# A two-layer decoder on one core: a batch's causal attention of the last block held until a later score unit of the wide text attention

## The chip, the cores and the metric

The kernel runs on one core of a Trainium2 chip. The metric is the device time of one execution in microseconds. Engines are called by their names: TensorE (PE in rows, its weight loads PEld), VectorE (DVE), ScalarE (ACT), GpSimd (POOL) and SyncE (SP), which starts the DMAs.

## The reference

Eight sequences of 112 tokens with 256 channels pass through two decoder layers of three blocks each, with a layer norm behind each block. The last two blocks matter here. Block 4 of the kernel's numbering is an attention to a text of 375 tokens with 16 heads 64 wide. Block 5 is a causal attention with 16 heads 16 wide, followed by a mixture of four experts. Cut to that, for every sequence b:

```python
def _L1_xattn_ref(x, cond, w_q, w_k, w_v, w_out, b_out):   # N_HEADS, D_HEAD = 16, 64
    attn = softmax(einsum('bqhd,bkhd->bhqk', q, k) * D_HEAD ** -0.5)
    return einsum('bhqk,bkhd->bqhd', attn, v).reshape(B, SQ, 1024) @ w_out + b_out

def _L1_ffn_ref(x, ...):                                    # HEADS, HD = 16, 16
    h = _rms(x, n1_w)
    q, k, v = _rms(heads(wq), qn_w), _rms(heads(wk), kn_w), heads(wv)
    attn = softmax(where(causal, q @ k.T * HD ** -0.5, -inf))
    x = x + zero_first_64((attn @ v) @ wo.T)
    xf = _rms(x, n2_w)
    return x + zero_first_64(sum(wts[:, e] * expert_e(xf)))

x = _layernorm(x + _L1_xattn_ref(x, ctx_768, ...))
x = _layernorm(x + _L1_ffn_ref(x, ...))
```

## The kernel before

The kernel is written as plans, one per stage. A plan is a list of units such as `("sc4", n)`, and every engine walks the same list and issues its own instructions of each unit, so the list is the order in all five queues. `step` says what a unit leaves on each engine's semaphore and a rough cost; `weave` (its loop is near the top of `build`) fills a list from several streams in turn: each stream is a generator that yields the units it wants placed, or `None` while it has to wait. `until(units)` yields `None` until these units stand in the list, and `rest(ns)` until the placed units' costs have grown by so much. These waits shape the order of the list alone. What an engine waits for on the chip is written in `tensor_s4`, `vector_s4` and so on, by semaphores.

Stage 4 is the one that matters. Its streams are woven by one call of `weave`:

```python
weave(s4_heads(), follow(s4_values, range(2, 2 * B)),
      follow(s4_out, range(B)), follow(s4_operands, range(B)), follow(s4_queries, range(2, B, 2)),
      follow(s5_operands, range(0, B, 2)), follow(s5_operands, range(1, B, 2)), s5_heads(), follow(s5_out, range(0, B, 2)),
      follow(s5_out, range(1, B, 2)),
      s5_split())
```

`s4_heads` places the wide heads of block 4: 64 score units `sc4`, eight per sequence b (HP = 8), each with two heads. A score unit is six matmuls on TensorE (L2604), two row maxima on VectorE (L2684) and two exponentials on ScalarE (L2653). One unit later `nm4` normalises on VectorE (L2691, L2695), two units later `trA4` and `trV4` transpose (TensorE L2612; copies on ScalarE L2645 and VectorE L2676), and three units later `av4` multiplies by the values (L2623). Behind eight of them, `s4_out` places `out` (16 matmuls with Wo, L398, in rows `psum<-w_Wo,s_attT`; on VectorE the sum and the moments, L636 to L645; on GpSimd one root, L693), then `norm` (L688) and `xT` (L587, L630), which turn the rows for block 5.

Block 5's attention of a sequence is placed among the units of later sequences. `s5_operands(b)`, which runs in one stream for even and one for odd b, places `rms5a` (ScalarE's sum of squares L2850, a copy on GpSimd L2978), `ms5a` (L2909, L2912, a root on GpSimd L2981), `qkv5` (twelve matmuls, L398, in rows `psum<-w_wq,x_ch`, `w_wk`, `w_wv`), `qkv5e` (ScalarE L2856 to L2859), `ms5` (VectorE's sums L2916 and L2919, then the reciprocal roots of all heads on GpSimd, L2985), after a rest `qk5` (VectorE's multiply with these roots, L2923), `qkT5` (four transposes, L2775) and `qkT5e` (ScalarE L2863 for q, VectorE L2929 for k). `s5_heads` then takes the sequence in four groups: two `s5` units (scores L2784, mask L2787) with a maximum per group, `mx5` (VectorE L2938), `s5e` (four exponentials, ScalarE L2871), `pT5` (four transposes L2793, a copy on VectorE L2943), two `av5` (L2803) and `oT5` (L2878). `s5_out` places `turn5` (L2810; VectorE L2949, L2951), `atT5` (L2815, L2882), `wo5` (L398, `w_wo,at5T`; L2956), `sqb5` (L2887), `msb5` (L2960; a root on GpSimd L2989), `xf5` (L2964; GpSimd L2993) and `xfT5` (L2825, L2892, L2895; GpSimd L2997). The units `split5` round the first experts' weights (L2831, L2836).

When all wide heads are placed, `ffnin` stands in the list: SyncE then loads the experts' weights, once the last `av4` is done. What is left of block 5's attention comes behind, and with the next stage the experts' matmuls (`psum<-xf,e_up` first), which need all of it. Score units are counted from 0 to 63.

Of the kernel before, what the change touches and what calls it, by code (L numbers as in the profile page):

```python
# [18 lines left out]
B, N, D = 8, 112, 256  # L19
# [11 lines left out]
HP = H // 2  # L31
# [126 lines left out]
def build(nc, ctx, a, out):  # L158
# [63 lines left out]
    def until(*units):  # L222
        while any(u not in placed for u in units):
            yield None

    def rest(ns):
        end = spent[0] + ns
        yield None
        while spent[0] < end and not hurry[0]:
            yield None  # L230
# [2203 lines left out]
    def until_banks(count):  # L2434

        while sum(all(name in r.value for r, name in freed) for freed in w4.freed) < count + 3:
            yield None
# [59 lines left out]
        return [("split5", name)]  # L2497

    def s5_operands(b):
        yield from until(("norm", 4, b), ("ones5",))  # L2500
        if b >= 2:
            yield from until(("turn5", b - 2))
        yield [("rms5a", b)]
        yield [("ms5a", b)]
        yield from until(("xTe", 4, b))
        yield from rest(REST / 2)
        yield from until_banks(2)
        rings["misc5"].take(("vv5", b), (A, ("v5", b)))
        yield [("qkv5", b)]
        yield [("qkv5e", b)]  # L2510
        yield [("ms5", b)]
        yield from rest(5500.0)
        if b == B - 1:
            yield from until(("pT5", b - 1, 1))
        yield [("qk5", b)]
        yield from rest(REST)
        yield from until_banks(1)
        yield [("qkT5", b)]
        yield [("qkT5e", b)]
# [57 lines left out]
    def s5_split():  # L2577
# [6 lines left out]
# [5 lines that stand above are left out]
# [869 lines left out]
```

## Time and profile before

| | us |
|---|---|
| median of 3 runs | 1171.46 |
| lowest and highest of them | 1166.77, 1177.46 |
| span of the profiled execution | 1165.0 |
| TensorE busy in it | 1001.8 (86%) |
| VectorE busy | 640.4 (55%) |
| ScalarE busy | 588.3 (50%) |
| GpSimd busy | 284.6 (24%) |

No time of the profiled execution other than its span is given. The busy shares are means over the whole program, in which this stage is about a third: the wide score units start at 661.7 us and the experts' first matmul at 1024.4. In timelines a row is a group of like instructions that follow each other: its start, how long it lasts, engine, line, operation, the tiles out and in, their shape, the count, and in brackets the idle time ahead of it with what ended it. Two rows of TensorE can overlap by some tenths, since matmuls are pipelined.

### The profile page before, as it was taken

What the parts mean: (1) busy time and instruction counts of PE and PEld (TensorE: products, weight loads), DVE (VectorE), ACT (ScalarE), POOL (GpSimd) and SP (SyncE); (2) the same over time, 40 slices, a digit from 0 to 9 for tenths busy, and PEclk for the clock granted to TensorE, in tenths of its full rate; (3) what the DMA queues carried; (4) which work ended last, traced back from release to release, by engine and by line L of the source; (5) the groups of instructions that cost most, each with busy time, mean ns of one, the idle gap of its engine ahead of it and who ended that gap; (6) DMA issues with size and microseconds to landing.
All of it is one profiled execution on the core that took longest, in us unless ns stands there. A gap on an engine that the chain in (4) does not pass through costs nothing.

```text
span 1165.0 us, 21556 instructions
## 1 busy us (share of the span) xinstructions
PE 1001.8 (86%) x8624; PEld 707.4 (61%) x8624; DVE 640.4 (55%) x1519; ACT 588.3 (50%) x1374; POOL 284.6 (24%) x292
## 2 busy tenths in 40 slices
PE   7996898887689988789998799889888897789995
PEld 4664565665388854456655676667666665447654
DVE  3246545666669833454455476776676664527003
ACT  5532565552468844344544354556555544465741
POOL 2521412100500033211112202221132124132733
PEclk9988889898989999899999988999999888679998
DMA  9341464102679785422252243313222105000001
GB/s 311 99 86 40 112 127 110 45 12 98 209 272 314 259 278 168 139 88 85 80 173 88 81 120 105 101 34 107 81 57 78 27 1 226 1 1 1 1 1 32
DMA packets 66676, 123.68 MB, mean 106 GB/s; under 512 B 11632, under 2 KB 41968, under 8 KB 62496
## 3 DMA queue, kind: packets, MB, share of 16 engines
q1 hardware_dynamic: 64528, 117.48, 33.0%
q0 software_dynamic: 2048, 4.82, 1.4%
q8 instruction: 68, 1.11, 0.4%
q14 instruction: 32, 0.26, 0.1%
HBM read 86.30 MB, written 35.92 MB: 105 GB/s over the span
## 4 chain that ended last, share of the span: by engine, by line
PE 56%; DVE 19%; ACT 11%; DMA 5%; issue 4%; POOL 4%; SPq 1%; another core or an unknown queue 0%; DVEq 0%; ACTq 0%; POOLq 0%
PE psum L398 38%; DVE s_p L2695 3%; ACT s_p L2653 3%; POOL rs L2985 2%; PE psum L2612 2%; DVE s_max L2684 2%; PE psum L2623 2%; PE psum L1369 2%; PE psum L2784 1%; DVE s_pT L2676 1%; PE psum L550 1%; DVE s_max L653 1%; PE psum L2173 1%; PE psum L2159 1%; PE psum L2604 1%
## 5 line engine op out<-in xcount | busy, mean ns | idle before, releaser
L2653 ACT ACTIVATE s_p<-psum,s_max 112x375 f32<-112x375 f32 x128 | 72.3, 569 | 87.6 <-DVE s_max L2684 87.6
L693 POOL TENSOR_TENSOR rstd<-meanvar,minus_half 112x1 f32<-112x1 f32 x40 | 23.1, 578 | 279.6 <-DVE meanvar L645 209.9
L653 DVE TENSOR_REDUCE s_max<-psum 112x2 f32<-112x750 f32 x64 | 59.4, 935 | 32.5 <-PE psum L550 31.4
L2985 POOL TENSOR_TENSOR rs<-ms,minus_half 112x32 f32<-112x32 f32 x8 | 43.5, 5442 | 110.3 <-DVE ms L2919 110.3
L398 PE MATMUL psum<-Wv,ctx 128*125 128x512 f16 x240 | 59.6, 392 | 11.2 <-ACT s_v L624 5.4
L398 PE MATMUL psum<-ctx,Wk 128*128 128x375 f16 x320 | 62.8, 331 | 5.0 <-ACT s_yT L2242 2.8
L2684 DVE TENSOR_REDUCE s_max<-psum 112x1 f32<-112x375 f32 x128 | 63.7, 539 | 2.3 <-PE psum L2604 2.1
L2612 PE MATMUL psum<-ident,s_p 112*125 112x112 f32 x384 | 61.4, 294 | 3.9 <-DVE s_p L2695 2.3
L609 ACT ACTIVATE s_k<-psum 128x375 f16<-128x375 f32 x64 | 31.2, 488 | 62.1 <-PE psum L398 59.5
L2604 PE MATMUL psum<-s_k,s_q 64*112 64x375 f16 x384 | 46.0, 345 | 17.0 <-ACT s_p L2653 6.5
L2612 PEld LDWEIGHTS psum<-ident,s_p 112*125 112x125 f32 x384 | 51.7, 198 | 13.7 <-DVE s_p L2695 3.9
L3303 POOL TENSOR_TENSOR hidden<-raw,hidden 128x448 f16<-128x448 f32 x44 | 45.6, 1036 | 54.4 <-ACT hidden L3186 52.7
L1431 ACT ACTIVATE s_pT<-psum 125x672 f32<-125x672 f32 x64 | 46.6, 730 | 22.8 <-PE psum L1357 21.2
L2623 PE MATMUL psum<-s_pT,s_v 125*64 125x112 f32 x768 | 53.9, 278 | 4.4 <-ACT s_attT L2661 4.4
L677 DVE SCALAR_TENSOR_TENSOR s_k<-psum,s_k 128x375 f16<-128x375 f32 x64 | 34.8, 546 | 36.2 <-ACT s_k L609 35.8
L624 ACT ACTIVATE s_v<-psum 125x512 f32<-125x512 f32 x48 | 28.3, 596 | 49.2 <-PE psum L398 33.4
L2623 PEld LDWEIGHTS psum<-s_pT,s_v 125*64 125x64 f32 x768 | 39.7, 143 | 20.1 <-issue 17.3
L398 PEld LDWEIGHTS psum<-Wv,ctx 128*125 128x125 f16 x240 | 32.1, 141 | 32.3 <-issue 9.6
L2695 DVE TENSOR_SCALAR s_p<-s_p,s_sum 112x375 f32<-112x375 f32 x128 | 49.3, 427 | 2.3
L3275 DVE SCALAR_TENSOR_TENSOR x_tok<-psum,wt,x_tok 112x192 f32<-112x192 f32 x32 | 12.6, 414 | 68.7 <-PE psum L398 68.6
L2645 ACT ACTIVATE s_pT<-psum 125x336 f32<-125x336 f32 x64 | 29.0, 453 | 38.3 <-PE psum L2612 38.2
L398 PE MATMUL psum<-x_ch,w_Wq 128*128 128x224 f32 x192 | 46.3, 382 | 2.1 <-ACT x_ch L630 1.5
(360 smaller groups left out, 2445.1 us busy)
## 6 DMA issues: line engine op xcount, KB each, us to landing
keys<-s_k SPq DMA_DIRECT2D x64, 187.5 KB, 2.2
s_k<-keys SPq DMA_DIRECT2D x8, 1500.0 KB, 7.6
values<-s_v SPq DMA_DIRECT2D x48, 224.0 KB
s_v<-values SPq DMA_DIRECT2D x16, 672.0 KB
raw_wg<-in_wg SPq DMA_DIRECT2D x8, 1024.0 KB, 6.6
raw_wu<-in_wu SPq DMA_DIRECT2D x8, 1024.0 KB, 7.1
raw_wd<-in_wd SPq DMA_DIRECT2D x8, 1024.0 KB
s_kd<-k_halves SPq DMA_DIRECT2D x48, 93.8 KB, 3.8
```

The source lines that it names most:

```text
L398: ins = TE.matmul(bank, left, right, start=i == 0, stop=last)
L653: VE.tensor_reduce(s1_max[b % 2][:, 2 * p:2 * p + 2], rings["s1"][unit][0:N, :, 0:S], X, ALU.max, negate=True).then_inc(*V.up("max1", n))
L677: VE.scalar_tensor_tensor(t[:, 1, :], rings["misc3"][unit][:, 0:S], 1 / WSCALE, t[:, 0, :], ALU.mult, ALU.subtract).then_inc(*V.up("k4", *at))
L1431: SC.activation(rings["pT1"][n], rings["s1"][unit][0:SCH, :, 0:NCH * N], ACT.Exp, scale=0.25).then_inc(*A.up("exp1", n))
L2604: ins = TE.matmul(rings["s4"][(n, j)][0:N, 0:S], q[rows, p, u, cols(b % 2)], k[rows, p, v, :], start=i == 0, stop=i == 2)
L2612: ins = TE.transpose(rings["t4"][unit][0:SCH, c * N:(c + 1) * N], p[:, c * SCH:(c + 1) * SCH], ident[0:N, 0:N])
L2623: ins = TE.matmul(rings["o4"][n // 4][64 * j:64 * j + 64, p % 4 * N:(p % 4 + 1) * N], s4_v[n // 4 % 3][:, c, 2 * (p % 4) + j, :], rings["p ...
L2653: SC.activation(rings["p4"][2 * n + j], rings["s4"][(n, j)][0:N, 0:S], ACT.Exp, bias=s4_max[b % 2][:, h:h + 1], accum_out=s4_sum[b % 2][:, ...
L2684: VE.tensor_reduce(s4_max[b % 2][:, h:h + 1], rings["s4"][(n, j)][0:N, 0:S], X, ALU.max, negate=True).then_inc(*V.up(name, n))
L2695: VE.tensor_scalar(t, t, sums[:, j:j + 1], None, ALU.mult).then_inc(*V.up(name, n))
L2985: GP.tensor_tensor(rs5[b % 2][:], ms5[b % 2][:], minus_half[:], ALU.pow).then_inc(*G.up("rs5", b))
L3303: GP.tensor_tensor(dst[:, 1, f, :], raw_, dst[:, 0, f, :], ALU.subtract).then_inc(*G.up("ll", *at))
```

## The change

One wait is added to the first line of `s5_operands`. It shapes the order of the list; no engine waits for another semaphore than before.

```diff
     def s5_operands(b):
-        yield from until(("norm", 4, b), ("ones5",))
+        yield from until(("norm", 4, b), ("ones5",), ("sc4", min(B * HP - 1, (b + 2) * HP + 2)))
         if b >= 2:
             yield from until(("turn5", b - 2))
         yield [("rms5a", b)]
```

A sequence's `rms5a`, and with it all that follows for that sequence in block 5's attention, now waits in the list for score unit 8(b+2)+2, at most 63: unit 18 for b = 0, 26 for b = 1, and 63 for b = 6 and 7. The other streams are as they were, and place their units around it.

The first place is TensorE's queue around b = 4's `qkv5`, in the steady part of the wide heads. The names: `s_p` and `s_pT` are the wide heads' probabilities and their transposes, `w_wq`, `w_wk`, `w_wv` block 5's weights, `w_Wo` block 4's output weights, `sc_n` and `pT_n` block 5's probabilities. Before, `qkv5` stands behind score unit 49:

```order
L2612 MATMUL psum<-ident,s_p_269 125x112 x3
L2612 MATMUL psum<-ident,s_p_270 125x112 x3
L2604 MATMUL psum<-s_k_237,s_q_262 112x375 x6
L398 MATMUL psum<-w_wq_245,x_ch 112x256 x2
L398 MATMUL psum<-w_wk_246,x_ch 112x256 x2
L398 MATMUL psum<-w_wv_247,x_ch 112x256 x2
```

and `out` of b = 5 two score units later, ahead of a transpose of block 5:

```order
L2623 MATMUL psum<-s_pT_272,s_v_238 64x112
L398 MATMUL psum<-w_Wo_241,s_attT 112x256 x8
L2793 MATMUL psum<-ident,sc_2_294 112x112 x4
L2803 MATMUL psum<-pT_0_296,v_1_288 32x112 x2
L2803 MATMUL psum<-pT_1_297,v_1_288 32x112 x2
```

After the change, TensorE has behind score unit 52:

```order
L2623 MATMUL psum<-s_pT_271,s_v_238 64x112
L2623 MATMUL psum<-s_pT_272,s_v_238 64x112
L2612 MATMUL psum<-ident,s_p_269 125x112 x3
L2612 MATMUL psum<-ident,s_p_270 125x112 x3
L2604 MATMUL psum<-s_k_237,s_q_262 112x375 x6
L398 MATMUL psum<-w_Wo_241,s_attT 112x256 x8
L398 MATMUL psum<-w_wq_245,x_ch 112x256 x2
L398 MATMUL psum<-w_wk_246,x_ch 112x256 x2
L398 MATMUL psum<-w_wv_247,x_ch 112x256 x2
L2623 MATMUL psum<-s_pT_273,s_v_238 64x112
```

The output product of b = 5 and the projections of b = 4 now follow each other in one unit.

The second place is VectorE's queue behind the last score unit, around the multiply of b = 7's q and k (`qk_1`) with its roots (`rs_1`); `ms_1` is the sum that GpSimd's roots are made of, `mx_0` and `pT_0` to `pT_3` belong to b = 6. Before:

```order
L2916 TENSOR_REDUCE ms_1_310<-sq_284 112x32
L2919 TENSOR_SCALAR ms_1_310<-ms_1_310,r_1_308 112x32
L2938 TENSOR_REDUCE mx_0_313<-psum 112x4 x2
L2960 TENSOR_SCALAR meanvar<-meanvar 112x1
L2938 TENSOR_REDUCE mx_0_313<-psum 112x4
L2943 COPY pT_0_296<-psum 112x448
L2964 TENSOR_SCALAR res<-x_tok,rstd 112x256
L2938 TENSOR_REDUCE mx_0_313<-psum 112x4
L2943 COPY pT_1_297<-psum 112x448
L2923 TENSOR_TENSOR qk_1_286<-qk_1_286,rs_1_312 112x512
```

After the change:

```order
L2938 TENSOR_REDUCE mx_0_313<-psum 112x4
L2943 COPY pT_0_296<-psum 112x448
L2938 TENSOR_REDUCE mx_0_313<-psum 112x4
L2943 COPY pT_1_297<-psum 112x448
L2943 COPY pT_2_298<-psum 112x448
L2916 TENSOR_REDUCE ms_1_310<-sq_284 112x32
L2919 TENSOR_SCALAR ms_1_310<-ms_1_310,r_1_308 112x32
L2943 COPY pT_3_299<-psum 112x448
L2923 TENSOR_TENSOR qk_1_286<-qk_1_286,rs_1_312 112x512
L2949 RECIPROCAL rd_0_315<-psum 112x16
L2951 TENSOR_TENSOR at_0_290<-psum,rd_0_315 112x256
L2956 TENSOR_TENSOR x_tok<-x_tok,psum 112x192
```

Seven rows of b = 5 and b = 6 stood between the sums of b = 7 (L2919) and its multiply (L2923); now one copy does, and the maxima and the other copies of b = 6 stand ahead of the sums.

The third place is TensorE's queue in the same stretch, around `qkv5` of b = 7. Before, it follows the transposes of b = 6's q and k (`qk_0`), and b = 6's scores come after it:

```order
L2810 MATMUL psum<-ident,oT_1_301 112x128 x4
L2815 MATMUL psum<-ident,at_1_291 128x112 x2
L2775 MATMUL psum<-ident,qk_0_285 128x112 x4
L398 MATMUL psum<-w_wq_245,x_ch 112x256 x2
L398 MATMUL psum<-w_wk_246,x_ch 112x256 x2
L398 MATMUL psum<-w_wv_247,x_ch 112x256 x2
L398 MATMUL psum<-w_wo_248,at5T_305 112x192 x2
L2784 MATMUL psum<-k_0_281,q_0_302 112x224 x4
L2787 MATMUL psum<-mask_306,ident_57 112x448 x2
```

After the change:

```order
L2784 MATMUL psum<-k_0_281,q_0_302 112x224 x4
L2787 MATMUL psum<-mask_306,ident_57 112x448 x2
L2810 MATMUL psum<-ident,oT_1_301 112x128 x4
L2784 MATMUL psum<-k_0_281,q_0_302 112x224 x4
L2787 MATMUL psum<-mask_306,ident_57 112x448 x2
L2793 MATMUL psum<-ident,sc_0_292 112x112 x4
L2825 MATMUL psum<-ident,res 128x112 x2
L398 MATMUL psum<-w_wq_245,x_ch 112x256 x2
L398 MATMUL psum<-w_wk_246,x_ch 112x256 x2
L398 MATMUL psum<-w_wv_247,x_ch 112x256 x2
L2793 MATMUL psum<-ident,sc_1_293 112x112 x4
```

Both `s5` units of b = 6 (`k_0`, `q_0`), a transpose of its probabilities and that of b = 4's output (`res`) have moved ahead of the projections of b = 7.

## Rows read from the trace of the kernel before

**Rows 1.** Busy time by stretches: us, then each engine's busy us, clock, DMA share, GB/s

```profile
836.00:875.40 39.40, 34.49 (x307) 25.21 (x306) 27.38 (x73) 22.23 (x73) 9.62 (x8) 0.96 0.27 79
...
960.85:1024.40 63.55, 44.80 (x282) 31.54 (x282) 27.62 (x59) 27.47 (x84) 20.17 (x17) 0.71 0.26 104
```

**Rows 2.** Timeline, TensorE, one batch among the wide heads: start, us, idle before

```profile
848.45 0.60 PE L2793 MATMUL psum<-ident,sc 112*112 112x112 f32 x4
...
853.63 3.71 PE L398 MATMUL psum<-w_Wo,s_attT 128*112 128x256 f32 x16
...
857.65 0.59 PE L2803 MATMUL psum<-pT,v 112*32 112x112 f32 x16
...
860.06 0.35 PE L2825 MATMUL psum<-ident,res 112*128 112x112 f32 x2
...
863.95 0.65 PE L2810 MATMUL psum<-ident,oT 128*112 128x128 f32 x4
...
867.23 0.55 PE L2775 MATMUL psum<-ident,qk 112*128 112x112 f32 x4
...
867.94 0.41 PE L2815 MATMUL psum<-ident,at 112*128 112x112 f32 x2 [0.17 <-ACT s_pT L2645]
...
871.30 0.69 PE L2604 MATMUL psum<-s_k,s_q 64*112 64x375 f16 x6 [1.19 <-DVE k L2929]
```

**Rows 3.** Timeline, TensorE, from the last score unit on

```profile
949.96 1.16 PE L2604 MATMUL psum<-s_k,s_q 64*112 64x375 f16 x6 [1.19 <-DVE k L2929]
...
960.78 1.12 PE L398 MATMUL psum<-w_wq,x_ch 128*112 128x256 f32 x4
...
962.59 1.03 PE L398 MATMUL psum<-w_wv,x_ch 128*112 128x256 f32 x4
...
972.38 0.59 PE L2803 MATMUL psum<-pT,v 112*32 112x112 f32 x16 [2.69 <-DVE pT L2943]
...
979.34 1.91 PE L398 MATMUL psum<-w_wq,x_ch 128*112 128x256 f32 x4
...
986.39 1.01 PE L2784 MATMUL psum<-k,q 32*112 32x224 f32 x8 [1.26 <-DVE k L2929]
987.34 0.58 PE L2787 MATMUL psum<-mask,ident 112*112 112x448 bf16 x2
...
1000.19 1.84 PE L2784 MATMUL psum<-k,q 32*112 32x224 f32 x8 [1.94 <-ACT e_up L2831]
...
1024.44 4.44 PE L398 MATMUL psum<-xf,e_up 128*128 128x448 f16 x12 [1.89 <-POOL xf L2997]
```

**Rows 4.** Timeline, VectorE, the same batch

```profile
847.11 0.62 DVE L2938 TENSOR_REDUCE mx<-psum 112x4 f32<-112x448 f32 x1 [6.04 <-PE psum L2787]
...
852.71 0.74 DVE L2695 TENSOR_SCALAR s_p<-s_p,s_sum 112x375 f32<-112x375 f32 x2
...
857.14 0.35 DVE L2964 TENSOR_SCALAR res<-x_tok,rstd 112x256 f32<-112x256 f32 x1 [2.25 <-POOL rstd L2989]
```

**Rows 5.** Timeline, GpSimd: roots of one batch among the heads, and of the last two

```profile
851.15 5.44 POOL L2985 TENSOR_TENSOR rs<-ms,minus_half 112x32 f32<-112x32 f32 x1 [19.21 <-DVE ms L2919]
...
970.81 5.44 POOL L2985 TENSOR_TENSOR rs<-ms,minus_half 112x32 f32<-112x32 f32 x1 [0.32 <-DVE ms L2919]
976.21 0.73 POOL L2993 TENSOR_TENSOR x_tok<-x_tok,x_in 112x256 f32<-112x256 f32 x1
...
987.20 5.44 POOL L2985 TENSOR_TENSOR rs<-ms,minus_half 112x32 f32<-112x32 f32 x1 [7.54 <-DVE ms L2919]
```

**Rows 6.** Timeline, VectorE, behind the last score unit

```profile
976.28 1.21 DVE L2923 TENSOR_TENSOR qk<-qk,rs 112x512 f32<-112x512 f32 x1 [2.05 <-POOL rs L2985]
...
994.52 0.68 DVE L2923 TENSOR_TENSOR qk<-qk,rs 112x512 f32<-112x512 f32 x1
```

**Rows 7.** The core's span and granted clock

```profile
core 0: 1165.0 us, clock 0.933
```

**Rows 8.** The line of the wide score matmuls: min/median/max ns, first and last start

```profile
L2604 PE MATMUL psum<-s_k,s_q x384: 317/322/561, 661.7 to 950.6; 64*112 64x375 f16 x192
```

## The prediction

> **What bounds the kernel now.** I read first the busy time by stretches, to find the stage that the change touches and how full each engine is in it; then TensorE's timeline of one batch there; then VectorE's and GpSimd's beside it; last the same engines behind the last score unit. The stage has two parts. While the 64 wide score units run, eight of them and the work of one batch of the last block fill 39.4 us, with TensorE busy for 34.5, VectorE for 27.4 and ScalarE for 22.2 [rows 1]: TensorE is 88% full, and what the others do mostly lies beside it. Behind the last wide value products, from 960.85 to 1024.40 us, TensorE is busy for 44.8 of 63.6 us and nothing else is full (VectorE 27.6, ScalarE 27.5), at a mean granted clock of 0.71, a mix of 2.4 and 1.2 GHz [rows 1]. There it is not the amount of work that sets the end, but the chain of the last batch, b = 7, through all engines, and what stands ahead of it in their queues. So work that leaves the first part is worth nearly its TensorE time, and what it costs in the second depends on whether it gets in front of that chain.
>
> **What moves.** Nothing is added or removed: the same units stand in both plans. The wait holds `rms5a` of a batch until score unit 8(b+2)+2; in the plan of before it stood at 8b+13 in the steady part, five units earlier. The units behind it had been held by rests as well, and so move less: `qkv5` of b = 4 goes from unit 49 to 52, its first `s5` from 55 to 58. That is three units, not eight. For b = 6 and 7 the wait is for unit 63.
>
> *First part, what leaves it.* Three units' worth of the last block is no longer placed before score unit 63. On TensorE: one transpose of probabilities (0.60 us), one value product (0.59), the turn of a batch's output (0.65), its second turn (0.41), the transposes of q and k (0.55) and those of the block's output (0.35) [rows 2], 3.15 us together. At 88% full that could be 3.6 us of time; I take -3, bounds 0 (if VectorE sets the pace in light units) and -3.6.
>
> *First part, what changes place.* Before, `qkv5` stands in one unit and the wide output product `out` two units later. Now they stand in one row, as the order above shows: `out` 3.71 us [rows 2], `qkv5` 2.84 (960.78 to the end of its third product, 962.59 + 1.03 [rows 3]), and the second half of `s5`, 1.01 + 0.58 [rows 3]: some 8.1 us in one unit. VectorE's maximum behind `s5` has all of it ahead; before, VectorE stood idle for 6.04 us there [rows 4], and now it has the sum behind `out` to do in the middle, so about as much. GpSimd's reciprocal roots, 5.44 us [rows 5], start now behind this clump and not ahead of `out`. Before, VectorE stood for 2.25 us for a root queued behind them [rows 4] while TensorE ran `out` (853.63 to 857.34 [rows 2]): that wait was covered. Now TensorE has in its place a score unit, transposes and a value product, some 4 us by the rows for these; still covered, but barely. If the cover is gone it is 2.25 us per batch on five batches, +11. `rms5a` and `ms5a` now stand in one unit, so VectorE waits for ScalarE's square where a unit lay between; `s5` covers that. On the other side, a score unit's matmuls waited 1.19 us for k (871.30 [rows 2]), once per batch; with `xT` gone from that unit ScalarE may be earlier: -6 over five batches at best. I take 0 for all of these, bounds -6 and +11; the nearest rows, the covered 2.25 and the exposed 1.19, pull against each other.
>
> SP's queue is unchanged: the loads for the experts start behind the last wide value product as before. Under GpSimd's 5.44 us VectorE's two normalising multiplies at 852.71 took 0.74 us together [rows 4, 5], so the sum has 0 for them. The Trainium skill, SBUF — State Buffer, section "Who interferes with whom", says that such a `tensor_scalar` can contend with GpSimd, and that whichever started first then blocks the other for its whole instruction. By that rule VectorE would have stood from 852.71 to 856.59, 3.9 us; the trace does not agree. A rival below takes the case up.
>
> *Second part.* I count from the last score unit's matmuls (949.96 [rows 3]). Ahead of `qkv5` of b = 7 TensorE had issued no `s5` of b = 6; now both halves and a transpose stand there, along with the 3.15 us from above, less the second turn of b = 5 (0.41). At full clock: 2 x 1.59 + 0.60 + 3.15 - 0.41 = 6.5 us; at half clock the first part of an `s5` is 1.84 us and not 1.01 (1000.19 against 986.39 [rows 3]), so up to 9. Behind the roots of b = 6 VectorE's queue has a maximum and a copy on which the next value product hangs: TensorE stands there for some 4 us where it stood 2.69 (972.38 [rows 3]), +1. So `qkv5` of b = 7, at 979.34 before [rows 3], comes 8 to 10 us later after the last score unit; I take 10. From there to its `s5` it was 1000.19 - 979.34 = 20.9 us [rows 3], with slack in it: 987.20 - 979.34 = 7.9 us until the roots start [rows 3, 5], of which the products of q and k are at most 2 x 1.91 = 3.8 [rows 3], so 4.0 for square, sums and VectorE's own queue; and 1.9 us from the roots' end (992.64 [rows 5]) to the multiply at 994.52 [rows 6]. Between 1.9 and 5.9 of it can be won, since VectorE now has one copy between sums and multiply; I take 4. Net +10 - 4 = +6 at `s5` of b = 7. From there to the first expert matmul it was 1024.44 - 1000.19 = 24.3 us [rows 3]. Now the outputs of b = 5 and b = 6 are both finished in it, with a wait for a root (2.25 [rows 4] where it stands open) ahead of the last turn: +1. Second part: +7. Bounds -4 (the roots of b = 6 started at 970.81 [rows 5], behind `out`; with `qkv5` of b = 6 ready earlier that chain can come forward as far as the slack above) and +14.
>
> **Sum.** -3 + 0 + 7 = +4 us. The profiled execution spans 1165.0 us [rows 7]; nothing else of its own time is given: 1169.0. The median of the runs shown, 1171.5, is 6.5 above that span, so in its terms the forecast is 1175.5. The three runs of before lie between 1166.8 and 1177.5; about 1% is what a measurement of this kernel can tell from no change.
>
> **Rivals.**
> *The roots stand open (slower).* The place is VectorE's queue behind the last score unit: the multiply of q and k right behind the sums, with 5.44 us of GpSimd between. Price: 9 us of extra half-clock work ahead of `qkv5`, +4 of idle TensorE in front of the value product, nothing won back, +1 at the end, +14; and 1 us per batch in the first part, +5. 14 + 5 - 3 = +16: 1187.5. It decides once `qkv5` of b = 7 starts over 10 us later after the last score unit. For it: before 976.28 VectorE already stood 2.05 us for such roots [rows 6]. Against: the slack of up to 5.9 us.
> *The gaps take it up (faster).* 18.8 us of idle TensorE in the second part [rows 1] hide all the deferred work and -3 stays; the wait for k goes (-6); the chain of b = 6 comes 4 us forward and carries through: -13, 1158.5. For it: the idle time. Against: it is made of waits inside one chain, and 1.84 us for 1.01 says that work put there costs more.
> *It does nothing.* The last batch's chain starts with `out` of b = 7 in either program, and a shift of three units cancels: 0, 1171.5. For it: the steady part has the same units per eight scores.
> *The roots block VectorE.* The multiply of q and k took 1.21 us beside GpSimd's add at 976.21 and 0.68 alone [rows 5, 6]. If whatever runs under the roots were held like that, 3.9 us per batch would fall where no `out` covers them: 6 x 3.9 = +23, 1194.5. Against: the 0.74 us of rows 4. The Trainium skill has this rule in SBUF — State Buffer, as above.
>
> **Chances.** Forecast 0.38, roots open 0.22, gaps 0.13, nothing 0.25, blocking 0.02. Faster by over 1% (under 1159.8): 0.10 of the gaps' case and 0.05 of the next two, 0.15. Slower by over 1% (over 1183.2): 0.18 of the open roots, the 0.02 and 0.05 of the forecast's upper side, 0.25. The rest, 0.60, is within 1%. The range 1160 to 1189 leaves out about 0.1 on either side.
>
> **What would show it.** From the first to the last score unit it was 949.96 - 661.7 = 288.3 us [rows 3, 8]; about 285 after, with VectorE's longest wait for a mask product still near 6 us. From the last score unit to the first expert matmul 74.5 us before; 81 to 82 after, with `qkv5` of b = 7 some 39 us after the last score unit and not 29.4, and VectorE idle for 3 to 5 us ahead of both last multiplies of q and k. Wrong if the second part stays at 75 us (then the gaps took it up) or if the first part grows.

## The result, and the profile of the changed kernel

The changed kernel takes 1187.55 us (median of 4 runs, 1180.41 to 1195.70), beside 1171.51 (4 runs) for the kernel before: a ratio of 1.0131, 95% interval 1.0082 to 1.0181, so about 1.3% slower. Two later repeats gave 1.0135 [1.0084, 1.0185] and 1.0069 [1.0031, 1.0106]; the medians differ by 16.0, 13.9 and 12.2 us. All ratios leave out executions over 1.5% above the fastest of the same kernel (four of 12 in again_before, two of 12 each in third_after, late_only and minus3). The forecast of 1175.5 (+4) had the right sign; the size is that of the rival it called "the roots stand open", 1187.5.

The changed kernel's core and stretches, as in [rows 7] and [rows 1] (us, then busy us of TensorE, weight loads, VectorE, ScalarE and GpSimd, granted clock, DMA share, GB/s). First the same 39.4 us as in rows 1, then a batch at a granted clock of 1.00 (score units 48 to 55), then the stretch that is called the second part there:

```profile
core 0: 1181.6 us, clock 0.920
```

```profile
836.00:875.40 39.40, 34.12 (x306) 25.26 (x306) 27.20 (x75) 22.41 (x76) 9.78 (x8) 0.96 0.27 80
887.61:927.33 39.72, 32.55 (x308) 24.16 (x308) 27.29 (x73) 21.91 (x74) 9.01 (x7) 1.00 0.19 57
972.10:1035.70 63.60, 47.73 (x293) 33.26 (x294) 27.57 (x59) 26.71 (x84) 17.91 (x14) 0.69 0.27 104
```

The second row is the one to remember: 39.72 us, of which TensorE works 32.55 and stands 7.2, at full clock. The line of the wide score matmuls [rows 8] now runs from 674.0 to 961.6:

```profile
L2604 PE MATMUL psum<-s_k,s_q x384: 317/322/561, 674.0 to 961.6; 64*112 64x375 f16 x192
```

So the stage begins 12.3 us later, though every instruction ahead of it is the same. From the first to the last score unit it is 961.22 - 673.99 = 287.2 us (288.3 before), and from there to the first expert matmul 80.4 (74.5 before). Taken at face value, most of the loss lies where the change does nothing. That is what the repeats had to settle.

TensorE behind the last score unit, which answers to [rows 3]:

```profile
961.22 0.69 PE L2604 MATMUL psum<-s_k,s_q 64*112 64x375 f16 x6
...
972.11 3.71 PE L398 MATMUL psum<-w_Wo,s_attT 128*112 128x256 f32 x16 [0.64 <-ACT s_attT L2661]
975.66 1.03 PE L398 MATMUL psum<-w_wq,x_ch 128*112 128x256 f32 x4
...
988.76 0.98 PE L2803 MATMUL psum<-pT,v 112*32 112x112 f32 x16 [4.08 <-DVE pT L2943]
...
993.42 1.84 PE L2784 MATMUL psum<-k,q 32*112 32x224 f32 x8
...
1000.64 1.92 PE L398 MATMUL psum<-w_wq,x_ch 128*112 128x256 f32 x4
...
1013.60 0.85 PE L2775 MATMUL psum<-ident,qk 112*128 112x112 f32 x4 [3.06 <-DVE qk L2923]
1015.93 1.83 PE L2784 MATMUL psum<-k,q 32*112 32x224 f32 x8 [1.47 <-ACT e_up L2831]
...
1041.60 3.86 PE L398 MATMUL psum<-xf,e_up 128*128 128x448 f16 x12 [1.89 <-POOL xf L2997]
```

`qkv5` of b = 7 starts 39.4 us after the last score unit (29.4 before), its `s5` 54.7 us after it (50.2 before). VectorE's last two multiplies of q and k, as in [rows 6], stand for the roots:

```profile
986.95 0.69 DVE L2923 TENSOR_TENSOR qk<-qk,rs 112x512 f32<-112x512 f32 x1 [3.37 <-POOL rs L2985]
...
1012.85 0.69 DVE L2923 TENSOR_TENSOR qk<-qk,rs 112x512 f32<-112x512 f32 x1 [4.92 <-POOL rs L2985]
```

GpSimd's roots, as in [rows 5]: one batch among the heads, with the single root queued behind it, and the last:

```profile
916.34 5.43 POOL L2985 TENSOR_TENSOR rs<-ms,minus_half 112x32 f32<-112x32 f32 x1 [7.04 <-DVE ms L2919]
921.75 0.55 POOL L2989 TENSOR_TENSOR rstd<-meanvar,minus_half 112x1 f32<-112x1 f32 x1
...
1007.38 5.44 POOL L2985 TENSOR_TENSOR rs<-ms,minus_half 112x32 f32<-112x32 f32 x1 [4.44 <-DVE ms L2919]
```

TensorE in the steady part (beside [rows 2]): a wait ahead of the score unit behind `s5`, and `out` and `qkv5` in one piece. VectorE there, as in [rows 4]:

```profile
939.50 0.69 PE L2604 MATMUL psum<-s_k,s_q 64*112 64x375 f16 x6 [1.55 <-DVE x_tok L2956]
...
943.36 3.71 PE L398 MATMUL psum<-w_Wo,s_attT 128*112 128x256 f32 x16 [0.20 <-ACT sc L2871]
946.91 1.03 PE L398 MATMUL psum<-w_wq,x_ch 128*112 128x256 f32 x4
```

```profile
911.97 0.62 DVE L2938 TENSOR_REDUCE mx<-psum 112x4 f32<-112x448 f32 x1 [3.30 <-PE psum L2787]
...
917.90 0.74 DVE L2695 TENSOR_SCALAR s_p<-s_p,s_sum 112x375 f32<-112x375 f32 x2
...
922.33 0.35 DVE L2964 TENSOR_SCALAR res<-x_tok,rstd 112x256 f32<-112x256 f32 x1 [2.24 <-POOL rstd L2989]
...
938.22 0.15 DVE L2909 TENSOR_SCALAR r<-r 112x1 f32<-112x1 f32 x1 [1.23 <-ACT junk L2850]
```

### The profile page after: what moved, and what is told of

It reads as the page before. It is cut to its first block, busy times and chain, and to the rows that moved or that the text cites. A ratio compares the mean times of both kernels' runs of the same rounds, so it can differ in the third digit from the quotient of the medians.

```text
span 1181.6 us, 21543 instructions
## 1 busy us (share of the span) xinstructions
PE 1013.2 (86%) x8624; PEld 712.7 (60%) x8624; DVE 639.3 (54%) x1519; ACT 586.1 (50%) x1374; POOL 283.5 (24%) x292
## 3 DMA queue, kind: packets, MB, share of 16 engines
q8 instruction: 68, 1.11, 0.4%
## 4 chain that ended last, share of the span: by engine, by line
PE 55%; DVE 20%; ACT 11%; DMA 5%; issue 4%; POOL 4%; SPq 1%; another core or an unknown queue 0%; DVEq 0%; ACTq 0%; POOLq 0%
PE psum L398 38%; ACT s_p L2653 3%; DVE s_p L2695 3%; DVE s_max L2684 2%; POOL rs L2985 2%; PE psum L1369 2%; PE psum L2612 2%; DVE s_pT L2676 1%; PE psum L2623 1%; PE psum L550 1%; DVE s_max L653 1%; PE psum L2784 1%; DMA raw_wg<-in_wg 1%; PE psum L2159 1%; PE psum L2173 1%
## 5 line engine op out<-in xcount | busy, mean ns | idle before, releaser
L398 PE MATMUL psum<-Wv,ctx 128*125 128x512 f16 x240 | 63.7, 413 | 13.4 <-issue 9.3
L2612 PE MATMUL psum<-ident,s_p 112*125 112x112 f32 x384 | 62.1, 297 | 6.2 <-DVE s_p L2695 3.2
L677 DVE SCALAR_TENSOR_TENSOR s_k<-psum,s_k 128x375 f16<-128x375 f32 x64 | 34.8, 546 | 37.3 <-ACT s_k L609 36.9
L2623 PEld LDWEIGHTS psum<-s_pT,s_v 125*64 125x64 f32 x768 | 39.0, 140 | 22.2 <-issue 19.2
L398 PEld LDWEIGHTS psum<-ctx,Wk 128*128 128x128 f16 x320 | 29.5, 101 | 30.6 <-issue 5.9
```

The lines of the kernel that those rows point to most:

```text
L398: ins = TE.matmul(bank, left, right, start=i == 0, stop=last)
L677: VE.scalar_tensor_tensor(t[:, 1, :], rings["misc3"][unit][:, 0:S], 1 / WSCALE, t[:, 0, :], ALU.mult, ALU.subtract).then_inc(*V.up("k4", *at))
L2612: ins = TE.transpose(rings["t4"][unit][0:SCH, c * N:(c + 1) * N], p[:, c * SCH:(c + 1) * SCH], ident[0:N, 0:N])
L2623: ins = TE.matmul(rings["o4"][n // 4][64 * j:64 * j + 64, p % 4 * N:(p % 4 + 1) * N], s4_v[n // 4 % 3][:, c, 2 * (p % 4) + j, :], rings["p ...
```

## The experiments

In all tables "units 16 to 63" is the time from the start of score unit 16 to that of unit 63, and "tail" that from there to the first expert matmul, each from the one profiled execution. Units 0 to 15 are left out because their instructions are the same in every kernel; what that hides is said behind the last run.

**The two kernels again, unchanged.** Was the late start of the stage the change's doing?

> The kernel before, unchanged, as a scale for everything else. Theory A (the change itself is worth 4 to 6 us, all in the last wide-attention stage; the other 12 us between the two profiled executions lie ahead of that stage, where both programs are the same, and are its wander): ratio 1.00, but the first wide score unit starts several us away from the 661.7 of the first profile, within some 655 to 680, and the stage itself, from the first score unit to the first expert matmul, repeats to 1 us: 362 to 364. Theory B (what is ahead of the stage belongs to the program and repeats with it): the first score unit again at 661 to 663.

> The changed kernel once more. Theory A: ratio 1.004 to 1.006; first score unit anywhere from 655 to 680; from it to the last one 287 us, from there to the first expert matmul 80 to 81. Theory B: ratio 1.013 again, with the first score unit again near 674.

| | ratio [95%] | stage starts | units 16 to 63 | tail |
|---|---|---|---|---|
| before, first profile | 1 | 661.7 | 226.5 | 74.5 |
| again_before | 0.9971 [0.9930, 1.0012] | 672.6 | 226.4 | 71.2 |
| after, first profile | 1.0131 [1.0082, 1.0181] | 674.0 | 230.0 | 80.4 |
| again_after | 1.0135 [1.0084, 1.0185] | 664.7 | 232.7 | 82.9 |

The order of the starts is reversed in the repeats, so the 12.3 us ahead of the stage are a difference between executions and nothing of the change's. The cost stays: about +5 among the score units and +9 behind them. The first profile had hidden the former: units 8 to 15, same code, took 28.8 us in it and 33.2 in the profile of before, where the granted clock was lower. Both rows, of before and then of after:

```profile
690.28:723.44 33.16, 30.13 (x227) 22.40 (x227) 22.06 (x59) 14.76 (x48) 7.23 (x11) 0.84 0.47 146
```

```profile
702.45:731.25 28.80, 25.63 (x227) 19.20 (x227) 22.14 (x59) 14.52 (x46) 7.22 (x11) 0.99 0.55 170
```

**late_only and early_only: the wait for half of the batches.**

```diff
-("sc4", min(B * HP - 1, (b + 2) * HP + 2)))
+*([("sc4", min(B * HP - 1, (b + 2) * HP + 2))] if b >= 4 else []))     # late_only
+*([("sc4", (b + 2) * HP + 2)] if b < 4 else []))                       # early_only
```

> The wait for the sequences b = 4 to 7 alone; those before are placed as in the kernel before, and all that stands behind score unit 63 is placed exactly as after the change. Theory A: the same cost behind the last score unit, 80 to 81 us to the first expert matmul, and no gain before it: 288 us between the score units; ratio 1.005. If the cost came from the early sequences: 74 to 75 us behind the last score unit and ratio 1.00.

> The wait for the sequences b = 0 to 3 alone: up to score unit 50 the list is that of the changed kernel, with the wide output product and the projections in one unit (28, 36, 44); behind it the sequences b = 4 to 7 follow without the wait. Theory C (the cost has two parts: up to 3 us among the score units, from the clump of the two products in one unit, and 6 to 9 us behind the last one, from work that came to stand there): 289 to 292 us between first and last score unit against 288, 76 to 80 behind it against 71 to 75, ratio 1.005 to 1.009. Theory D (the cost is all behind the last score unit): 288 or less between them.

late_only: ratio 0.9999 [0.9962, 1.0036], units 16 to 63 224.2 us, tail 78.4. early_only: 0.9999 [0.9965, 1.0033], 231.6 us, tail 74.1. The tail's cost belongs to the late batches: with the wait on them alone it is there (78.4), without it not. Among the score units early_only's profile is 5 us longer than that of before and late_only's is not. Those 5 us are clock, though: of its 231.6 us TensorE is idle for 25.5 (26.1 in before) and busy for 206.1 (200.4), at a mean granted clock of 0.94 (0.98). In units 16 to 47, where its list is the changed one, idle TensorE did rise, from 16.2 to 19.9 us; in units 48 to 63, where it turns back to the other, it fell from 9.8 to 5.6. late_only's profile is that of its longest execution (1187.34 us), so its stretches count for less; last2 below puts the same question again. early_only's ratio, which by these stretches should have been about 1.004, fits once units 0 to 15 are counted: they took 56.0 us in its profile and 61.7 in that of before.

**ahead: the last projections put in front again.** `s5` of b = 6 is held until `qkv5` of b = 7 stands in the list.

```diff
-                                   and (b < 2 or ("atT5e", b - 2) in placed))
+                                   and (b < 2 or ("atT5e", b - 2) in placed)
+                                   and (b != B - 2 or g > 0 or ("qkv5", B - 1) in placed))
```

> The change as it is, with one more rule: the scores of b = 6 wait in the list for the projections of b = 7, so that these stand ahead of them again. Theory A (6 us of the tail are lost because the projections of b = 7 stand behind both score units of b = 6, and GpSimd's 5.44 us of roots then stand open): the projections come some 30 us after the last score unit and not 39.4, VectorE is not idle for 4.9 us ahead of the last multiply of q and k, and the first expert matmul comes 74 to 76 us after the last score unit and not 80.4; time 5 us below again_after, ratio to before 0.998 to 1.001. Rival (the tail is longer because there is more TensorE work in it, wherever it stands): 79 to 81 us, as after the change.

Ratio 1.0132 [1.0087, 1.0178]. VectorE's 4.92 us ahead of the last multiply are gone, `qkv5` of b = 7 starts at 35.3 us and not 39.4, and the tail is still 79.7 us (80.4 in after, at the same mean clock of 0.72), with `s5` of b = 7 56.5 us after the last score unit (54.7 in after). So that wait is not what costs: TensorE's idle time in the tail is 23.2 us without it and 22.9 to 23.0 in the three profiles of the change, against 19.2 in both of before. The work that stands in the tail costs much the same ahead of or behind the last projections; other places were not tried.

**minus3, minus2, minus1: the wait at other units.** The `+ 2` of the change becomes -1, 0 or +1.

```diff
-("sc4", min(B * HP - 1, (b + 2) * HP + 2))
+("sc4", min(B * HP - 1, (b + 2) * HP + (-1)))     # minus3; (0): minus2; (1): minus1
```

> The same wait with 3 score units less: unit 8(b+2)-1. In the steady part only the squares and the root of a sequence come later, its projections and all that follows stand where they stood before, and so does nearly all behind the last score unit. Theories C and D: 288 us between the score units, 72 to 75 behind, ratio 0.999 to 1.002. If it is the squares and their root that cost (they stand in one unit now): ratio 1.005 or more.

> The wait with 2 score units less, unit 8(b+2): projections one unit later than before, in a unit of their own, the wide output product in the next; behind the last score unit the projections of b = 7 stand ahead of the scores of b = 6, as before, with one unit's worth of work more. Theory C: no clump, so 288 us between the score units; 74 to 77 behind; ratio 1.001 to 1.004. Rival (any delay costs as much as the whole change): 1.01.

> The wait with 1 score unit less, unit 8(b+2)+1: projections two units later, in one unit with the wide output product, ahead of it; behind the last score unit the projections of b = 7 stand behind the scores of b = 6, as after the change, with two units' worth of work more. Theory C: 289 to 292 us between the score units, 77 to 81 behind; ratio 1.007 to 1.010. If the clump costs nothing: 287 to 288 and ratio 1.005.

| | ratio [95%] | units 16 to 63 | tail |
|---|---|---|---|
| minus3 | 1.0040 [1.0002, 1.0077] | 232.6 | 72.8 |
| minus2 | 1.0121 [1.0075, 1.0166] | 233.3 | 72.3 |
| minus1 | 1.0103 [1.0049, 1.0158] | 235.9 | 75.1 |
| the change (+2) | 1.0131, 1.0135, 1.0069 | 230.0, 232.7, 230.2 | 80.4, 82.9, 83.2 |

There is no slope that leads from before to after. Only the change clearly pays in the tail. Among the score units all four take longer, but not for one reason: TensorE is idle there for 30.4 us in minus2, 34.8 in minus1 and 30.1 to 31.5 in the change, and for 26.9 in minus3, where before has 26.1; minus3's 6 us are TensorE's busy time at a lower clock (205.7 us at 0.95, 200.4 at 0.98 before). So minus2's order costs idle time where minus3's hardly does, which goes the way of the ratios; why minus2 measures as much as the whole change these profiles don't say.

**last2: the wait on batches 6 and 7 alone.** Up to unit 60 its list is that of before.

```diff
+*([("sc4", B * HP - 1)] if b >= B - 2 else []))
```

> The kernel before, with the wait for the last score unit on batches 6 and 7 alone. Its list is that of before up to unit 60, rms5a of batch 6 stands behind unit 63 and the list behind it is that of minus3. Theory G (the tail's cost comes from the three units' work that batches 4 and 5 leave behind, and holding batches 6 and 7 does nothing by itself): units 16 to 63 take 226 to 228 us, the tail 71 to 75, ratio 0.998 to 1.003. Rival H (holding back rms5a of batch 6 and so its chain is itself the cost): the tail takes 79 or more, ratio 1.005 to 1.010.

Ratio 0.9990 [0.9956, 1.0025], units 16 to 63 227.9 us, tail 74.9: theory G. Holding these two costs nothing; with late_only's 78.4 us that leaves, by elimination, the work of batches 4 and 5 as what costs in the tail.

**unclump: `out` and `qkv5` in different units again.** The prediction's first worry.

```diff
         yield from rest(REST / 2)
+        if 2 <= b < B - 1:
+            yield from until(("s5", b - 2, 1))
         yield [("out", 4, b)]
```

> The changed kernel with one edit: the wide output product out of batches 2 to 6 also waits until the second half of s5 of two batches earlier stands in the list. So out, and with it norm, xT and xTe, stand one unit later (in the steady part out in unit 8k+5, with qkv5 still in 8k+4), and nothing else up to score unit 63 moves. Theory E (the part of the cost that falls among the score units, +5.6 us in units 16 to 63, comes from out and qkv5 standing in one unit): units 16 to 63 take 227 to 229 us instead of 232, the time from the last score unit to the first expert matmul stays at 80 to 83, ratio to the kernel before 1.007 to 1.010. Rival F (it is the granted clock and the order of all the rest, whatever stands beside out): units 16 to 63 stay at 231 to 234, ratio 1.012 to 1.016. Above 1.018: xT and xTe, a unit later, now stand in the way of the k of the score units.

Ratio 1.0123 [1.0070, 1.0177], units 16 to 63 234.0 us, tail 83.2: rival F. In the steady part its units 52 and 53 take 6.8 + 7.2 us; with the clump they take 9.9 + 4.2 (third_after, below), all four at a granted clock of 1.00. The clump costs nothing. The 234.0 us were run at a lower clock (0.95, the change 0.96 to 0.97); at 1.00, units 32 to 39 take 42.4 us without the clump and 42.3 with it.

**third_after: the change once more.**

> The changed kernel again, without an edit, beside the two others. If the cost is +5 to +6 us among the score units and +8 to +9 behind them, its ratio lies at 1.012 to 1.015 and its profile shows 230 to 234 us in units 16 to 63 and 79 to 83 us in the tail. If the cost read so far was chance of the executions looked at, the ratio falls under 1.008.

Its profile is where it was expected (230.2 us, tail 83.2), its ratio is not: 1.0069 [1.0031, 1.0106], which by what was expected above would speak for chance. The two other measurements, and ahead, which has the same list among the score units, say 1.013. The interval leaves out 1, the medians are 12.2 us apart, and with its two longest executions counted the means give 1.009; I read it as a cost at the lower end, some 0.7 to 1.3%, and not as none.

The profiles of last2 and third_after have a batch of the steady part (score units 48 to 55) at a granted clock of 1.00 in either list, which the profiles of before did not have there. First last2, then third_after:

```profile
875.09:912.82 37.73, 32.80 (x307) 24.19 (x306) 27.39 (x73) 22.21 (x73) 8.93 (x7) 1.00 0.22 68
```

```profile
879.43:919.15 39.72, 32.54 (x307) 24.15 (x306) 27.30 (x73) 21.93 (x74) 9.01 (x7) 1.00 0.20 59
```

The same work, the same clock, 2.0 us more: TensorE stands for 7.2 us per batch where it stood for 4.9. VectorE's rows in third_after say for what:

```profile
890.33 0.15 DVE L2909 TENSOR_SCALAR r<-r 112x1 f32<-112x1 f32 x1 [1.23 <-ACT junk L2850]
...
914.15 0.35 DVE L2964 TENSOR_SCALAR res<-x_tok,rstd 112x256 f32<-112x256 f32 x1 [2.24 <-POOL rstd L2989]
```

The first is `ms5a`, which now stands in one unit with `rms5a` and waits for ScalarE's square; behind it in VectorE's queue stands the work that TensorE waits for at the next score unit:

```profile
891.61 0.69 PE L2604 MATMUL psum<-s_k,s_q 64*112 64x375 f16 x6 [1.55 <-DVE x_tok L2956]
...
908.76 0.69 PE L2604 MATMUL psum<-s_k,s_q 64*112 64x375 f16 x6 [0.93 <-DVE meanvar L2960]
...
915.09 0.60 PE L2793 MATMUL psum<-ident,sc 112*112 112x112 f32 x4 [1.08 <-DVE pT L2943]
...
917.80 0.59 PE L2803 MATMUL psum<-pT,v 112*32 112x112 f32 x16 [1.19 <-DVE pT L2943]
```

The second is the root that GpSimd has behind the 5.44 us of reciprocal roots; the copies that TensorE waits for at 915.09 and 917.80 stand behind it. At 908.76 it waits for a row of VectorE that stands behind the sums of `ms5` (L2916 and L2919, some 0.9 us of VectorE's own time).

**two_waits: these two waits taken out by place alone.** `enter_unit` is the old body of `place`. Two units are entered in the list later, all else stays word for word as in the change: `ms5a` one score unit behind `rms5a`, and `ms5` behind `msb5` of two batches earlier, which is in the same unit. The second move changes two things, the order of GpSimd's roots and that of VectorE's sums.

```diff
+        if what == "ms5a" and at[0] < 6:
+            held_back.setdefault(("sc4", (at[0] + 2) * 8 + 3), []).append(unit)
+        elif what == "ms5" and 2 <= at[0] < 6:
+            held_back.setdefault(("msb5", at[0] - 2), []).append(unit)
+        else:
+            enter_unit(unit)
```

> The changed kernel with two units moved in its list, everything else word for word in place: ms5a of each batch but the last two stands one score unit behind rms5a and no longer right behind it, and ms5 of batches 2 to 5 stands behind msb5 of two batches earlier in the same unit, so that GpSimd's single root goes ahead of the 5.44 us of reciprocal roots. In the changed kernel at full granted clock a batch of the steady part took 39.7 us with 7.2 us of idle TensorE (third_after, score units 48 to 55), before 37.7 with 4.9 (last2). Theory J (the first part's cost is idle time behind these two waits of VectorE's queue, 1.23 us for ScalarE's square and 2.24 us for the root): both waits fall under 0.5 us, a batch of the steady part at full granted clock takes 37 to 38.2 us, units 16 to 63 take 225 to 229 us, the tail stays at 80 to 84, ratio 1.004 to 1.009. Rival K (TensorE waits for something else that these two waits only hide): the two waits go and the batch stays at 39.2 us or more, ratio 1.010 to 1.015.

| | ratio [95%] | units 16 to 63 | units 48 to 55, clock 1.00 | tail |
|---|---|---|---|---|
| two_waits | 1.0012 [0.9980, 1.0045] | 225.6 | 37.41 | 79.1 |

```profile
883.28:920.69 37.41, 32.74 (x307) 24.19 (x307) 27.77 (x73) 21.94 (x74) 9.17 (x7) 1.00 0.21 61
```

```profile
896.13 0.14 DVE L2922 TENSOR_SCALAR r<-r 112x1 f32<-112x1 f32 x1
...
914.40 0.35 DVE L2977 TENSOR_SCALAR res<-x_tok,rstd 112x256 f32<-112x256 f32 x1
```

Neither row has a wait in brackets any more (13 lines further down here: L2922 is L2909, L2977 is L2964). The batch is back at 37.4 us with 4.7 of idle TensorE. Over units 16 to 63 TensorE's idle time is 24.9 us, where the change has 30.1 to 31.5. The first profile of the change has the same granted clocks in all six stretches of eight units (0.95, 0.91, 1.00, 0.92, 1.00, 1.00); beside it the two moves are worth 4.4 us (225.6 for 230.0), though units 40 to 47 took 0.6 us more. Theory J, with a ratio even below its 1.004.

Both moves were made in one run, so the shares come from the profile alone: the unit with the square's wait went from 5.7 to 4.1 us, the three behind `ms5` (units 53 to 55) from 14.6 to 13.6. TensorE's 1.55 us are down to 0.49, its 0.93 and 1.08 us are gone, but ahead of the two value products it stands as long as before or longer (0.54 and 1.19 us in third_after):

```profile
914.54 0.59 PE L2816 MATMUL psum<-pT,v 112*32 112x112 f32 x16 [1.04 <-DVE pT L2956]
...
919.33 0.59 PE L2816 MATMUL psum<-pT,v 112*32 112x112 f32 x16 [1.30 <-DVE pT L2956]
```

So it isn't shown how much of the gain is the root's and how much the later sums'. Nor are the two waits the only way to idle time: minus2's profile has VectorE wait for the square (1.23 us) and not for the root, and TensorE's 30.4 us; minus3's has both (1.47 and 2.24 us) and 26.9. No version beat the kernel before by more than its interval.

**The whole stage, units 0 to 15 included.** From the first score unit to the first expert matmul, with units 0 to 15 in brackets (us):

| | whole stage | ratios |
|---|---|---|
| before | 362.7 (61.7), 359.3 (61.6) | 1, 0.9971 |
| last2 | 358.8 (56.0) | 0.9990 |
| two_waits | 360.7 (56.0) | 1.0012 |
| early_only | 361.7 (56.0) | 0.9999 |
| late_only | 364.7 (62.1) | 0.9999 |
| minus1, minus3, minus2 | 367.0 (56.0), 367.1 (61.6), 367.3 (61.7) | 1.0103, 1.0040, 1.0121 |
| the change | 367.6 (57.3), 377.2 (61.6), 369.4 (56.0) | 1.0131, 1.0135, 1.0069 |
| ahead | 370.4 (57.0) | 1.0132 |
| unclump | 373.2 (56.0) | 1.0123 |

All that measure as before lie under 365 us and all that measure slower at 367 or more. Units 0 to 15, the same code throughout, differ by 6 us with the clock, and both profiles of before had them slow; a comparison that leaves them out shows early_only and two_waits as slower than their ratios.

## Why the prediction was right in sign and short in size

**The work that leaves the first part: right.** The step said 3.15 us of TensorE leave the score units. Of each order there is a profile that shows each eight units at a granted clock of 1.00 (us, and TensorE's busy us in brackets):

| score units | order of before | order of after |
|---|---|---|
| 16 to 23 | 31.28 (28.32), before | 31.60 (27.54), again_after |
| 24 to 31 | 40.58 (36.35), before | 37.09 (33.32), third_after |
| 32 to 39 | 40.70 (36.56), before | 42.31 (37.00), after |
| 40 to 47 | 37.72 (32.81), last2 | 40.64 (32.97), ahead |
| 48 to 55 | 37.73 (32.80), last2 | 39.72 (32.55), after |
| 56 to 63 | 33.63 (28.70), before | 33.89 (28.99), after |
| sum | 221.6 (195.5) | 225.3 (192.4) |

TensorE's work fell by 3.2 us. That the time would fall with it did not happen.

**"I take 0 for all of these", the change of place: this is the step that failed.** Idle TensorE grew from 26.1 to 32.9 us, +6.8, so these six stretches cost +3.6 at equal clock and not -3; with the clock as granted, the means of the profiles are 226.5 before (two) and 231.0 after (three), +4.5. "If the first part grows" was one of the prediction's own signs of being wrong. The value was inside its bounds of -6 and +11, but 0 was argued wrong in two sentences. "`s5` covers that", of `ms5a` behind `rms5a`: `s5` covered a part, and 1.23 us of VectorE's wait came out as 1.55 on TensorE. "Still covered, but barely", of the root: VectorE's wait is 2.24 us (2.25 before), but `out` no longer runs beside it, and TensorE stands 1.08 us for a copy right behind it. I had priced that as 2.25 us per batch if the cover were gone, and put it at nothing. A third piece the step didn't have: `ms5`'s sums now stand ahead of what a score unit waits for (0.93 us at 908.76). two_waits shows that these places are what costs: with both waits gone and the sums later, at the same order otherwise, 4.4 us go at the same clocks (5.4 of the mean, 231.0). How they share it is not shown. Against that, the wait for k (1.19 us, [rows 2]) did go, as the step allowed.

**The clump: right that it costs nothing, wrong on what it does.** VectorE's longest wait for a mask product did not stay near 6 us; it is 3.30 (911.97). unclump shows the clump to be harmless.

**The second part, +7: right in its steps, not in its reason, and a little small.** Every step has its row in the first profile. `qkv5` of b = 7 was put at 39 us: 39.4. TensorE standing for some 4 us: 4.08 (988.76). VectorE idle 3 to 5 us ahead of both multiplies: 3.37 and 4.92. `s5` of b = 7 +6: +4.5. From there to the first expert matmul +1: 25.7 us for 24.3, +1.4. The tail was put at 81 to 82: 80.4, +5.9 in this pair of profiles. Over the profiles it is 82.2 (80.4, 82.9, 83.2) against 72.9 (74.5, 71.2), +9.3; last2, with nearly the list of before, had 74.9, so it may be 7 to 9. Of the +9.3, 3.8 us are TensorE's idle time (19.2 to 23.0) and 5.6 its busy time (53.7 to 59.3 in the mean, at 0.72 and 0.70), which is more than the 3.15 us that moved. The reason given, that the work costs because it gets in front of b = 7's chain, did not hold: ahead put `qkv5` of b = 7 back to 35.3 us, and its `s5` came later still (56.5). Nor is the wait named in the rival, VectorE's multiply behind the sums, the cause: ahead took it away and kept the tail.

**Sum.** 4.5 + 9.3 = +13.8 us by the profiles of the two kernels, 12.2 to 16.0 by the medians. The whole stage, units 0 to 15 included, says +10.4 (361.0 to 371.4), since those units, the same code, were faster in two of the three profiles of the change. Forecast: -3 + 0 + 7 = +4. The sign is the second part's alone, as the first part went the other way, and the result lies 1.4 us inside the upper end of the range, which was set for a rival.

**The rivals.** The open roots' 16 us were near the total, and their "1 us per batch" was the right kind: roots that stand open in the score units. Their part of 14 us in the tail was too much, and its reason fell with ahead. "It does nothing" fell on both parts. "The gaps take it up" fell both ways. "The roots block VectorE" fell too: at 917.90, under GpSimd's 5.43 us from 916.34 on, the two normalising multiplies took 0.74 us together, as in rows 4, and both last multiplies of q and k took 0.69, with no GpSimd add beside them. The blocking that the Trainium skill describes for `tensor_scalar` beside GpSimd (SBUF — State Buffer, "Who interferes with whom") is not borne out by these rows either, but it is by others. In the changed kernel VectorE's two multiplies at 928.05 took 1.10 us and not 0.74; the first had started 0.1 us ahead of an instruction of GpSimd and took 0.41 us, as it does alone; the second started at 928.38, while that instruction ran, took 0.77 us and ended 0.2 us behind it:

```profile
928.05 1.10 DVE L2695 TENSOR_SCALAR s_p<-s_p,s_sum 112x375 f32<-112x375 f32 x2
```

```profile
928.16 0.77 POOL L2997 TENSOR_TENSOR xf<-xf,xf 128x224 f16<-128x224 f32 x1 [4.68 <-ACT xf L2895]
```

Each of the two first profiles has three such pairs, so it cost the same on either side. The order counts as well: at 822.14 of before VectorE's multiply of q and k had started first and took its 0.68 us, and GpSimd's add behind it took 1.11 us where it takes 0.73 alone. Beside the roots the rule fails: 30 of these normalising multiplies ran wholly within the roots' 5.44 us in the two first profiles, and each took 0.41 to 0.42 us. What sets the roots apart, no run here shows.

**Open.** Which of the pieces left over from b = 4 and 5 makes the tail longer, since ahead only showed that their place ahead of or behind the last projections does not matter; how the first part's cost is shared between the square, the root and the sums; and why minus2 costs as much as the whole change.

## What to carry to other kernels

When a unit moves, follow what stands behind it in the queue of each engine that waits, and ask of every wait that was covered what runs beside it in the new place: here a new wait of 1.23 us on VectorE, an old one of 2.24 that TensorE's long product had covered, and 0.9 us of sums in a new place went with 2 us per batch. Compare stretches at the same granted clock, eight units at a time and from several executions, before a difference of a few us is believed, and look at the engine's idle time beside its busy time: a longer stretch with the same idle time is clock and not order. And where a cost is a wait inside one queue, swapping two neighbours in the list can win it back: two moves went with a ratio of 1.001 where the change alone had 1.007 to 1.013.

## What the hardware showed that I had not expected

The start of the stage, behind some 660 us of identical instructions, wandered from 658.7 to 675.9 us over the fourteen profiles of this study, and neither kernel was tied to an end of it (before 661.7 and 672.6; after 674.0, 664.7 and 666.9). Single stretches with the same instructions did so by their clock: units 8 to 15 took 33.16 us at 0.84 and 28.80 at 0.99. Behind the first expert matmul, where all kernels are the same again, it was 140.0 to 144.7 us. On a single core that is as large as the whole effect looked for, so that one profile of each kernel put 12.3 us of 16.6 in the wrong place.
